# Running the first experts' hidden units between the last attention weights: the seam of a two-part kernel laid out anew

## What is computed

```
W = (1e-4 + |q - k|)^-2 for 16 heads of 64;  W /= 1e-4 + rowsum(W)
x += (gate * (W @ v)) @ W_out + b_out
h = relu(x @ W1[e] + b1[e]) for 8 experts of 512;  the two best experts of each token
x += sum over the two of weight * (h @ W2[e] + b2[e])
x += linear attention (16 heads of 8, relu(q), relu(k), decays) @ W_o + b_o
x += x~ with the 384 best tokens of 512 replaced by gelu(x~ @ w_block)
```

## Time and profile before

| | us |
|---|---|
| median of 3 runs | 1534.47 (1534.38 to 1539.09) |
| profiled execution | 1535.58 |
| its span, first to last instruction | 1533.8 |
| TensorE busy | 1460.3 |
| ScalarE busy | 1035.5 |
| VectorE busy | 989.5 |
| GpSimd busy | 819.6 |

### The profile page before, as it was taken

The page is one execution under the profiler, slowest core; times in us unless marked ns, Lnnn a source line. Parts: engine busy times, 40 slices in busy tenths (PEclk is TensorE's granted clock), DMA queues, the critical chain, the costliest instruction groups (busy, mean ns, idle before and its releaser), DMA issues.

```text
span 1533.8 us, 18468 instructions
## 1 busy us (share of the span) xinstructions
PE 1460.3 (95%) x6704; PEld 809.2 (53%) x6704; DVE 989.5 (65%) x2083; ACT 1035.5 (68%) x831; POOL 819.6 (53%) x681
## 2 busy tenths in 40 slices
PE   6999999999999999999999999789999999999974
PEld 4544554545545444454454445346666666666643
DVE  4766766766676677567667666664466575675664
ACT  1789868977978878878968987934454555555531
POOL 5578878879879978987987888730000000000000
PEclk8999999999999999999999999999999999999995
DMA  3001011001001101101001001532011010010100
GB/s 108 1 15 23 15 28 37 15 16 49 16 16 29 35 16 29 36 15 29 22 21 36 16 15 36 142 130 99 1 63 56 7 63 29 35 62 1 63 7 7
DMA packets 45851, 55.16 MB, mean 36 GB/s; under 512 B 13824, under 2 KB 32512, under 8 KB 44608
## 3 DMA queue, kind: packets, MB, share of 16 engines
q1 hardware_dynamic: 45760, 53.97, 11.7%
HBM read 49.11 MB, written 4.85 MB: 35 GB/s over the span
## 4 chain that ended last, share of the span: by engine, by line
POOL 44%; PE 36%; issue 12%; DVE 6%; DMA 1%; POOLq 0%; SPq 0%; ACT 0%; DVEq 0%
POOL wsum L297 17%; PE y L1040 14%; PE z L74 11%; POOL wsum L294 9%; POOL sq_l L286 5%; POOL hT L303 5%; POOL sqk L280 4%; POOL sqq L276 2%; POOL sq_h L284 2%; DVE w L510 2%; PE sc L376 1%; PE sc L371 1%; PE tb L976 1%; PE av L389 1%; PE pj L74 1%
## 5 line engine op out<-in xcount | busy, mean ns | idle before, releaser
L510 DVE TENSOR_SCALAR w<-sc,k 128x512 f32<-128x512 f32 x512 | 348.8, 743 | 148.3 <-PE sc L376 120.1
L596 ACT ACTIVATE w<-w 128x2048 f32<-128x2048 f32 x128 | 237.6, 1904 | 194.4 <-DVE w L510 194.0
L297 POOL TENSOR_TENSOR wsum<-wsum,w 128x512 f32<-128x512 f32 x256 | 328.5, 1283 | 20.1
L878 ACT ACTIVATE hr<-z,b 128x512 f32<-128x512 f32 x256 | 175.6, 686 | 238.1 <-PE z L74 238.0
L1040 PE MATMUL y<-hr,w 128*128 128x512 f32 x512 | 261.5, 593 | 0.0
L376 PE MATMUL sc<-query,key 64*128 64x512 f32 x1024 | 243.9, 595 | 0.0
L389 PE MATMUL av<-w,vt 128*64 128x512 f32 x1024 | 236.8, 605 | 6.6 <-DVE gT L517 4.8
L600 ACT ACTIVATE w<-w 128x2048 f32<-128x2048 f32 x128 | 240.3, 1901 | 0.4
L604 ACT ACTIVATE w<-w 128x2048 f32<-128x2048 f32 x128 | 239.8, 1897 | 0.0
L74 PE MATMUL z<-xs_h,w_h 128*128 128x512 f32 x256 | 201.4, 787 | 0.1
L294 POOL TENSOR_TENSOR wsum<-w 128x512 f32<-128x512 f32 x128 | 164.4, 1284 | 8.8 <-ACT w L604 8.8
(11 more groups left out here) (166 smaller groups left out, 2167.5 us busy)
## 6 DMA issues: line engine op xcount, KB each, us to landing
hT<-head_recips SPq DMA_DIRECT2D x64, 256.0 KB, 4.0
rb<-routing SPq DMA_DIRECT2D x8, 2048.0 KB, 7.2
w<-in_W SPq DMA_DIRECT2D x16, 256.0 KB, 4.9
xa<-in_X SPq DMA_DIRECT2D x8, 256.0 KB, 4.2
xc<-in_X SPq DMA_DIRECT2D x8, 256.0 KB, 2.8
x<-xc SPq DMA_DIRECT2D x8, 256.0 KB, 4.0
out<-prod SPq DMA_DIRECT2D x8, 256.0 KB, 2.3
x<-x SPq DMA_DIRECT2D x1, 1792.0 KB, 10.6
```

The lines of the kernel that those rows point to most:

```text
L297: nc.gpsimd.tensor_tensor(wsum[:, u, :], wsum[:, u, :], w[:, j % 2, u, c, :], ALU.add).then_inc(s_added, 1)
L510: nc.vector.tensor_scalar(w[:, s, 2 * r + v, c, :], sc[:, i, v, :], k2[:, s, r, c, v:v + 1], 0.0, ALU.add, ALU.max).then_inc(s_d2, 1)
L596: nc.scalar.activation(w[:, j % 2, u, :, :], w[:, j % 2, u, :, :], ACT.Sqrt).then_inc(s_sqrt, 1)
L878: nc.scalar.activation(hr[:, n % HR, :], z[:, n % 2, :], ACT.Relu, bias=b1[:, n % NU:n % NU + 1]).then_inc(S["hr"], 1)
```

## The change

The tiles of the second half are put in another order, and the split first-layer weights become two pairs of tiles, one for experts 0 to 3 and one for 4 to 7. A small tile `room` is added before `w`, so that everything up to `yT` ends ahead of `w`; the second-layer weights `w2` and `rb0` now lie in the first slot of `w`.

SyncE loads all first-layer weights at once and the second layer only when quad 30 has been added and gated; the spreading of the routing goes ahead of the normalizer of quad 30. ScalarE does relus 0 to 8 between the logarithms and powers of quad 31. TensorE moves `turn_f(0)` ahead, moves the two groups of weighted values of quad 31 to steps 1 and 7, `turn_routing(0)` from before hidden product 2 to before 4, and sums and outputs to later steps. VectorE splits experts 0 and 1 between the last eviction slots, puts `front_norm(0)` before the last slot, and moves the gate multiplies, `reciprocals(NQ - 2)` and what follows them into the steps.

```diff
@@ -113,6 +113,8 @@
         std = sb("std", [P, NC])
         rstd = sb("rstd", [P, NC])
         holder = sb("holder", [P, 1])
+
+        room = sb("room", [P, 64])
 
         w = sb("w", [P, 2, 4, NC, T])
 
@@ -679,19 +681,21 @@
 
 
         w1 = sb("w1", [P, NE, FF])
-        w2 = sb("w2", [P, NE * NF, D])
-        hr = sb("hr", [P, HR, T])
+        HE = NE // 2
+        w1s_early = [sb("w1_h_early", [P, HE, FF], F32R), sb("w1_l_early", [P, HE, FF], F32R)]
         x_first = sb("x_first", [P, NC, D])
-        rwT = sb("rwT", [NE, T])
-
-        w1s = [sb("w1_h", [P, NE, FF], F32R), sb("w1_l", [P, NE, FF], F32R)]
-
-        xs = [sb("xs_h", [P, 2, T], F32R), sb("xs_l", [P, 2, T], F32R)]
         xn_f = sb("xn_f", [P, NC, D])
         xT_f = sb("xT_f", [P, T])
+        xs = [sb("xs_h", [P, 2, T], F32R), sb("xs_l", [P, 2, T], F32R)]
+        rwT = sb("rwT", [NE, T])
+
+        w1s_late = [sb("w1_h_late", [P, HE, FF], F32R), sb("w1_l_late", [P, HE, FF], F32R)]
+        hr = sb("hr", [P, HR, T])
         ye = sb("ye", [P, T])
+        yT = sb("yT", [P, T])
+
+        w2 = sb("w2", [P, NE * NF, D])
         rb0 = sb("rb0", [P, NE, T])
-        yT = sb("yT", [P, T])
 
         x = sb("x", [P, B * NC, D])
         rb1 = sb("rb1", [P, NE, T])
@@ -747,6 +751,8 @@
         in_w2 = [ctx.enter_context(nc.semaphore(f"s_in_w2_{e}")) for e in range(NE)]
         NU = NE * NF
         AHEAD = 6
+
+        EARLY = 9
         front_loads = [
             (wr[:, :], a["Wr"]), (br[:, :], a["br"].partition_broadcast(P)),
             (etri[:, :, :], a["c_etri"]), (b1[:, :], a["b1"]), 
@@ -774,6 +780,9 @@
 
         nat = "p (c d) -> p c d"
 
+        def w1s(e, columns=slice(None)):
+            return [w[:, e % HE, columns] for w in (w1s_early, w1s_late)[e // HE]]
+
         def front_bank(f):
 
             return y[:, 1, :] if f == 0 else fa[:, :]
@@ -784,18 +793,18 @@
         def _(sp):
             normalizer, store_x1 = att_sync(sp)
 
-            def load_experts(es):
-                for e in es:
+            def load_first_layer():
+                for e in range(NE):
                     sp.dma_start(w1[:, e, :], a["W1"][e]).then_inc(in_w1[e], 16)
+
+            def load_second_layer():
+                for e in range(NE):
                     sp.dma_start(w2[:, e * NF:(e + 1) * NF, :], a["W2"][e].rearrange("(k p) d -> p k d", p=P)).then_inc(in_w2[e], 16)
 
             def spread_routing(f):
                 sp.wait_ge(S["rwT"], f + 1)
                 sp.dma_start(rwd[f % 2], rwT[:, :]).then_inc(S["rwd"], 16)
                 sp.wait_ge(S["rwd"], 16 * (f + 1))
-                if f == 0:
-                    sp.wait_ge(att["added"], 12 * (NQ - 1))
-                    sp.wait_ge(att["gated"], 2 * (NQ - 1))
                 sp.dma_start(rb[f % 2][:, :, :], rwd[f % 2].partition_broadcast(P)).then_inc(S["rb"], 16)
 
             def store(t):
@@ -806,12 +815,14 @@
             sp.dma_start(x_first[:, :, :], x1[0]).then_inc(S["in_x"], 16)
             for dst, src in front_loads:
                 sp.dma_start(dst, src).then_inc(S["in_front"], 16)
-            load_experts(range(0, 4))
+            load_first_layer()
             normalizer(NQ - 3)
-            load_experts(range(4, NE))
+            sp.wait_ge(att["added"], 12 * (NQ - 1))
+            sp.wait_ge(att["gated"], 2 * (NQ - 1))
+            load_second_layer()
             sp.dma_start(b2[:, :], a["b2"].rearrange("e d -> d e"), allow_slow_non_contiguous=True).then_inc(S["in_b2"], 16)
+            spread_routing(0)
             normalizer(NQ - 2)
-            spread_routing(0)
             sp.wait_ge(att["added"], 12 * NQ)
             sp.wait_ge(att["gated"], 2 * NQ)
             sp.dma_start(x[:, 0:(B - 1) * NC, :].rearrange("p (b c) d -> p b c d", c=NC),
@@ -895,8 +906,6 @@
                         turned_o1(t)
                     if k == 31:
                         root_t(t, 1)
-                if (b, k) == (0, 2):
-                    turned_routing(0)
                 if f < B:
                     if k == 17:
                         root_f(f)
@@ -906,21 +915,33 @@
                         exponential(f)
                     if k == 30:
                         turned_routing(f)
-                if b < B:
+                if b < B and b * NU + k >= EARLY:
                     hidden(b * NU + k)
 
             square_roots, logarithm, power = att_scalar(act)
+            root_f(0)
             square_roots(NQ - 1)
-            root_f(0)
             nc.scalar.preload_act_table_set("natural_log_exp_and_others")
             logarithm(NQ - 1, 0)
-            for u in range(4):
-                if u < 3:
-                    logarithm(NQ - 1, u + 1)
-                if u == 3:
-                    exponential(0)
-                power(NQ - 1, u)
+            logarithm(NQ - 1, 1)
             act.wait_ge(S["in_front"], 16 * len(front_loads))
+            hidden(0)
+            hidden(1)
+            power(NQ - 1, 0)
+            exponential(0)
+            hidden(2)
+            hidden(3)
+            power(NQ - 1, 1)
+            hidden(4)
+            logarithm(NQ - 1, 2)
+            turned_routing(0)
+            hidden(5)
+            hidden(6)
+            power(NQ - 1, 2)
+            hidden(7)
+            logarithm(NQ - 1, 3)
+            hidden(8)
+            power(NQ - 1, 3)
             for b in range(B + 2):
                 if b == 1:
                     act.wait_ge(S["in_tail"], 16 * len(tail_loads))
@@ -1025,7 +1046,7 @@
                     pe.wait_ge(S["hr"], n - 1)
                 if b == 0 and k % NF == 0:
                     pe.wait_ge(S["w1s"], 2 * (k // NF) + 2)
-                product(nc, z[:, n % 2, :], [w[:, k // NF, (k % NF) * P:(k % NF + 1) * P] for w in w1s],
+                product(nc, z[:, n % 2, :], w1s(k // NF, slice(k % NF * P, (k % NF + 1) * P)),
                         [v[:, b % 2, :] for v in xs]).then_inc(S["z"], 1)
 
             def expert(n):
@@ -1071,13 +1092,17 @@
                         logits(f)
                     if k == 24:
                         turn_routing(f)
-                if (b, k) == (0, 0):
+                if (b, k) == (0, 1):
+                    weighted_values(NQ - 1, 0)
+                if (b, k) == (0, 7):
+                    weighted_values(NQ - 1, 1)
+                if (b, k) == (0, 10):
                     sums(NQ - 1)
-                if (b, k) == (0, 2):
+                if (b, k) == (0, 13):
                     output(NQ - 2)
-                if (b, k) == (0, 14):
+                if (b, k) == (0, 22):
                     output(NQ - 1)
-                if (b, k) == (0, 16):
+                if (b, k) == (0, 25):
                     turn_output(B - 1)
                 if b < B:
                     n = b * NU + k
@@ -1086,15 +1111,13 @@
                         hidden(n + AHEAD)
 
             weighted_values, sums, output, turn_output = att_tensor(pe)
+            turn_f(0)
             sums(NQ - 2)
             output(NQ - 3)
             pe.wait_ge(S["in_front"], 16 * len(front_loads))
-            turn_f(0)
             logits(0)
-            weighted_values(NQ - 1, 0)
-            weighted_values(NQ - 1, 1)
             for n in range(AHEAD):
-                if n == 2:
+                if n == 4:
                     turn_routing(0)
                 hidden(n)
             for b in range(B + 2):
@@ -1250,9 +1273,10 @@
 
             def split_w1(e):
                 dve.wait_ge(in_w1[e], 16)
-                V.tensor_copy(w1s[0][:, e, :], w1[:, e, :]).then_inc(S["w1s"], 1)
+                hi, lo = w1s(e)
+                V.tensor_copy(hi, w1[:, e, :]).then_inc(S["w1s"], 1)
                 dve.wait_ge(S["w1s"], 2 * e + 1)
-                V.tensor_tensor(w1s[1][:, e, :], w1[:, e, :], w1s[0][:, e, :].bitcast(F32), ALU.subtract).then_inc(S["w1s"], 1)
+                V.tensor_tensor(lo, w1[:, e, :], hi.bitcast(F32), ALU.subtract).then_inc(S["w1s"], 1)
 
             def weigh(g):
                 b, e = g // NE, g % NE
@@ -1322,46 +1346,49 @@
                         expert_ranks(f)
                     if k == 26:
                         routing(f)
-                if (b, k) == (0, 5):
-                    sums(NQ - 1)
-                if (b, k) == (0, 6):
-                    output(NQ - 2)
+                if (b, k) == (0, 2):
+                    weighted_values(NQ - 1, 0)
                 if (b, k) == (0, 8):
                     dve.wait_ge(S["in_b2"], 16)
-                    dve.wait_ge(att["added"], 12 * NQ)
+                    weighted_values(NQ - 1, 1)
                 if (b, k) == (0, 9):
+                    reciprocals(NQ - 2)
+                if (b, k) == (0, 12):
+                    sums(NQ - 1)
+                if (b, k) == (0, 14):
+                    output(NQ - 2)
+                if (b, k) == (0, 20):
                     reciprocals(NQ - 1)
-                if (b, k) == (0, 19):
+                if (b, k) == (0, 23):
                     output(NQ - 1)
```

(25 more changed lines are left out.)

## The result

The changed kernel took 1554.49 us (median of 4, 1553.11 to 1556.35) against 1536.03 for the kernel before in its runs: a ratio of 1.0119 with a 95% interval of 1.0097 to 1.0140, 18 us slower. I had forecast 1539.4, range 1531 to 1546.

The account below looks back on a forecast made before the run. The prediction took TensorE, busy 95% of the span, as the bound. Terms -1.8 + 1.5 + 0.5 + 4.4 + 0.3 = +4.9 us, put on the median of 1534.47, gave 1539.4 us, range 1531 to 1546.

Parts of the forecast that it names:

- Sign: Whole kernel: forecast slower by 4.9 us; chances 0.52 slower, 0.36 same, 0.12 faster.
- turn 1: TensorE's turn of batch 1's rows, wanted at T + 17.2; 4.0 us forecast lost there, and 0.4 more in handing over.
- step 2: VectorE's splits 0 and 1 between eviction slots: 6.2 us contended, TensorE losing 3.2 us before the last distances; bounds 0 to 3.2.
- step 3: First norm ahead of VectorE's last eviction: 3.0 us, not 1.2, so the third square root starts at 984.0.
- Hidden product 4: TensorE's product behind the routing's transposes: forecast at 1005.3; with weighted values still owed, 1.8 us ahead of the old kernel.
- The stop before the routing: TensorE stands some 9.9 us after hidden product 3 for VectorE's routing chain; half clock behind it costs 1.5.
- step 8: Quad 30's reciprocals behind the last gate multiply: batch 1's norm ends at T + 21.2, costing TensorE 4.4 us; bounds 0 to 6.
- T: The start on TensorE of weighted values (31, 1), from which the forecast counted the late reciprocals' chain.
- Step 9: Last output and x's store nine steps later: tail loads wanted at step 0 of batch 1, 0.3 us; bounds 0 to 1.5.
- The clock rival: Three more thin stretches (974.8, 985 to 993, before turn 1) could each cost 1.5 us: +8, 1542.5; chance 0.20.
- The quiet port: Early splits and norm at the seam uncontended by GpSimd: -4.5 us, with x quick -5, 1529.5; chance 0.13.
- the harmless reciprocals: Late reciprocals of quad 30 cost near nothing before turn 1: +0.5 us, 1535.0; chance 0.22.

Follow-up runs that it names:

- e4_splits_back: Changed kernel with the splits of experts 0 and 1 moved behind the hand-over and the first norm behind the last slot: 1551.45 us, ratio 1.0110.
- e1_tail_early: Changed kernel with SyncE issuing the tail loads ahead of the store of the last x1 tile: 1545.07 us, ratio 1.0070.
- e5_recip: Changed kernel with quad 30's reciprocals behind the first routing, its normalizer ahead of the routing's spreading, batch 1's statistics ahead of output 30's addition: 1550.56 us, ratio 1.0103.
- e2_act_wait: Changed kernel with ScalarE's wait for the tail loads moved from ahead of unit 32's relu to step 16 of batch 1: 1544.36 us, ratio 1.0068.
- e3_out31_later: Changed kernel with VectorE adding the last output at step 26, not 23, and the turned output and its addition one step later: 1547.16 us, ratio 1.0090.
- e11_both_ends: Changed kernel with tail loads ahead of x1's store and the last output behind batch 1's routing, nothing else: 1540.84 us, ratio 1.0033.

## Why the prediction was wrong

*Sign and mechanisms ahead of turn 1: right.* Splits (step 2): 6.2 forecast, 6.07 measured and not 7, the stop 3.2 against 2.84. What their early place cost the kernel, with the norm's, was not separable from nothing (`e4_splits_back`). Norm (step 3): 3.0 against 4.37, mis-sized (4.37 to 4.48 in the eight profiles with the norm at this place or ahead of the gate multiply); each of its four instructions can wait for an addition; the time fits about three such waits, which no row shows one by one. Hidden product 4: forecast 1005.3, measured 1007.43, less 1.78 is 1005.65. The stop before the routing: 9.9 against 8.32 with the clock down behind it. Reciprocals (step 8): the reciprocal ran at T + 5.0 (1025.02 to 1030.05), the norm ended at T + 21.1 against T + 21.2, and TensorE lost 3.16 and 0.25, not 4.4; x was ready 9.9 us after its issue, past the 9 that I had allowed it but within the bound, and came 1.1 us later than the chain. At turn 1 the forecast was +4.6 and the mark says +3.9, for the most part because the reciprocals' step was 1.0 too dear.

*Step 9 failed.* I wrote that the tail loads are wanted at "step 0 of batch 1" and priced their delay at 0.3, at most 1.5. That is TensorE's wait. ScalarE and VectorE wait for the same loads at the start of their batch 1, and ScalarE's batch 1 begins when TensorE is at step 26 of batch 0, since it makes relus six units ahead. Moved nine steps back, the loads were some 8 us too late there, not 0.3: 7.08 us of stop and half clock behind it, shown by two experiments that took the lateness away from either side.

*A wait was not seen at all.* Step 9 also moved VectorE's addition of the last output to its step 23, ahead of batch 1's softmax at 24. I asked of that move what waits for the output, not what stands behind it in VectorE's order: 2.58 us, and the clock behind it. In the kernel before the addition stood at step 19, ahead of a gap, and held nothing up.

*The clock rival* was half right. Two of the three thin stretches that I named did end at half clock (0.50 at 980 to 982, 0.54 at 996 to 998), but that time fell into the waits behind them: in `e1_tail_early` the clock was 1.00 through both, and the routing's transposes stood at 41.74 us from the common mark, against 41.75 here. Behind turn 1's stop the clock stayed up in this profile and fell in others. What cost time were two stops that I had not seen. (Its price was added up wrong too: three more times 1.5 is +9.4, not +8.)

*The quiet port and the harmless reciprocals* both fell: no split beside quad 30's additions escaped, and TensorE lost 3.16 and 0.25 us at turn 1, of which the edits of `e5_recip` took away some 2.

The size, 18 us against 5, is thus 13 to 14 us at the end of batch 0; the kernel without these two losses measured +5.1.

## What to carry to other kernels

When a transfer is moved later, look up every engine's wait for it, and put each at the time of the unit that it holds, not at the step number: an engine that works six units ahead meets "the start of the next batch" six units early. When an instruction is moved past others on an in-order engine, price what stands behind it as well as what it waits for. And a wait for a long chain (here the routing) belongs at the last place in the order where its result is used: moving one such wait was worth 6 to 7 us and, with the four other losses gone, decided the sign of the whole change.

## What the runs showed of the hardware

The first half's length, by the same code, differed from one profiled execution to the next: its mark of quad 31's second slot stood anywhere from 958.76 to 966.56 us in thirteen profiles. They differ already in the first 50 us: the granted clock at 20 to 30 us was 0.50 to 0.83 among them and at 40 to 50 us either 0.83 or 1.00. These two don't put the marks in order, though: the latest mark goes with 0.68 and 1.00. For an edit at the seam the distance from a common mark is therefore the sharper measure, and differences of 2 us between medians are not to be believed without it.

That distance has a scatter of its own. Five profiles with the same code up to turn 1 (the changed kernel, `e1_tail_early`, `e2_act_wait`, `e3_out31_later`, `e11_both_ends`) reached it 80.4 to 82.6 us behind the common mark. A stretch in which TensorE hardly stops repeats far better: from turn 1 to the end five kernels took 493.3 to 493.5 us.

The length of a stop alone didn't tell whether the clock fell behind it. Stops of 1.97 us (`e11_both_ends`, at 1043.13) and 2.58 us were followed by half clock. Of two stops at the same place, ahead of turn 1, the one of 3.13 us in `e1_tail_early` was (0.62 and 0.52 at 1044 to 1048) and the one of 3.16 us in the changed kernel was not (1.00 throughout).

A group of four short VectorE instructions that take 1.12 us together with GpSimd quiet (`xn_f`, 128x128 each) took 4.37 to 4.39 us beside GpSimd's additions of 1.3 us each (seven profiles), and 3.02 to 3.19 beside a single product of GpSimd of 2.35 us (three profiles). Instructions of 32 elements paid as well: 0.81 us for `pr` at 998.71 in the changed kernel, 0.19 at 1063.04.
